# Decoder layer on one core: two more tiles of x copied in and split ahead of the context, the first half of the values' weights ahead of tiles 6 and 7, four column sums behind the weights' split

## Chip, core and metric

The kernel runs on 1 core of one Trainium2 chip. The metric is the device time of one execution in microseconds (us), lower is better.

## What is computed

One decoder layer over x (2 batches x 2048 rows x 512 columns, float32): a self-attention without softmax, a cross-attention to a context of 2 x 154 rows with a mask and a softmax over 16 heads, and a feed-forward step with a gate that mixes each row with the row before it; after each of the three the input is added and the rows are normalised.

```
x = layernorm(x + self_attn(x))            # (q k^T) v, no softmax: no row-by-row score is needed
x = layernorm(x + cross_attn(x, ctx, ctx, mask))   # softmax(q k^T / sqrt(32)) v, 16 heads
x = layernorm(x + ffn(x))                  # sigmoid(xr W_r) * (relu(xk W_k)^2 W_v)
```

Since the self-attention has no softmax, the kernel folds it for each batch into one matrix made of the Gram matrix x^T x and the sums of x's columns. The change is in the part that collects these two and that projects the context to the keys and values of the cross-attention.

## The kernel before

The program has two blocks, `prologue` and `layers`. The prologue (from the start to about 116 us) reads x by rows in 32 tiles of 128 rows, 16 a batch (`HALF`), through a ring of 4 buffers (`RING`). Tile j uses buffer j % 4. Every product with full precision is made of three passes over a high and a low part of each operand, so data that has come in is first split: ScalarE rounds it to the high part, VectorE subtracts that from the raw data.

The program of each engine is written out by hand, in order, and engines meet by semaphores only.

SyncE (`sp_program`) issues the copies. `load(j)` (L188) copies tile j, 256 KB. From tile 4 on it waits until the tile that was in the same buffer has been split (`split_lo`), halved (`halved`) and added to the column sums (`summed`). All copies of SyncE stand in one queue, in program order: tiles 0 to 3, the context (L192, 616 KB), tiles 4 to 7, the first half of the values' weights (L195, 512 KB), the second half (L196, 512 KB), the keys' weights (L197, 1024 KB), the values' bias broadcast to 128 rows (L198), the column biases (L199), then tiles 8 to 19.

ScalarE (`act_program`): `high(j)` makes the high part of tile j (L220) and half of the tile (L221). `part_high(i)` (L245) makes the high part of piece i of what the context's products need: 0 is the context, 1 and 2 are the halves of the values' weights, 3 is the keys' weights. The order is tiles 0 to 4, piece 0, tiles 5 to 7, pieces 1 to 3; then ScalarE issues four copies on its own queue (self_wv, self_bv, self_wk, cross_wq, 1024 KB each except the bias), splits tiles 8 to 11 and copies the keys out of PSUM (L260).

VectorE (`dve_program`): `low(j)` first adds tile j to the column sums `x_sum` (L301, for tiles 0 to 19), then makes the low part of the tile (L305). `part_low(i)` (L335) makes the low part of piece i. The order is tiles 0 to 4, piece 0, tiles 5 to 7, pieces 1, 2, 3, tiles 8 and 9, then the values with their bias out of PSUM (L347, `v_raw`, which gives `v_sum`), then tiles 10 to 17.

GpSimd sums the columns of tiles 20 to 31; its first add waits for tile 19's.

TensorE (`pe_program`): nine warming products, `sums(0..7)` (tiles 0 to 7 into the Gram matrix, L442 and L447), the three products of the values (they wait for `part_lo` of the pieces 0 to 2), the four products of the keys (they wait for piece 3; the second, third and fourth also each wait for one of the three `v_raw` additions, whose PSUM bank they take), then `sums(8..17)` and the rest of the prologue. The products use lines 88 to 90 (`three_pass`). The column sums are read by TensorE only once a batch (`columns`, L464).

`layers` is the main part: 16 groups of 256 rows, a hand-written pipeline over all engines from 116 us to the end. It is not changed.

Of the kernel before, what the change touches and what calls it, by code (L numbers as in the profile page):

```python
# [12 lines left out]
KT = D // P  # L13
# [10 lines left out]
RING = 4  # L24
# [58 lines left out]
def f32(ap):  # L83
    return ap.bitcast(F32)
# [20 lines left out]
def prologue(nc, io, mem, banks, weights, kv, m_in, xt, x_ring, place):  # L105
# [8 lines left out]
    x_in, x_both, x_lo = zip(*x_ring)  # L114
# [4 lines left out]
    ctx_t, w_k, w_v, bv_row, v_raw, x_sum = (place[x] for x in ("ctx_t", "cross_wk", "cross_wv", "bv_row", "v_raw", "x_sum"))  # L119
# [4 lines left out]
    to_split = [[x[:, k, :] for x in whole[i]] for i, k in  # L124
                ((0, slice(0, KT)), (1, slice(0, KT // 2)), (1, slice(KT // 2, KT)), (2, slice(0, KT)))]
# [5 lines left out]
    rows_of = [(r, min(P, B * CTX - r)) for r in range(0, B * CTX, P)]  # L131
    TILES = B * S // P
    HALF = TILES // B
    vector_adds = range(HALF + RING)
    wide = lambda name: io[name].rearrange("(k p) n -> p k n", p=P)
    early = ("cross_wq",) + LATE_WEIGHTS[:-1]

# [19 lines left out]
    with ExitStack() as ctx:  # L157
        flag = lambda name, per=1, step=1: Flag(nc, ctx, name, per, step)
        ctx_in, wv_in, wv_rest_in, wk_in = (
            flag(x, 1, 16) for x in ("ctx_in", "cross_wv_in", "cross_wv_rest_in", "cross_wk_in"))  # L160
        biases_in, ones_set = flag("cross_biases_in", 2, 16), flag("ones_set")
        part_in, part_hi, part_lo = (ctx_in, wv_in, wv_rest_in, wk_in), flag("ctx_parts_hi", 4), flag("ctx_parts_lo", 4)
        x_here = [flag(f"gram_x{i}", 1, 16) for i in range(RING)]
        split_hi, split_lo, halved, summed, gram_mm = (
            flag(x) for x in ("gram_hi", "gram_lo", "gram_half", "gram_sum", "gram_mm"))
        made, zeroed = flag("ident_zeroed"), flag("zeroed", 2)
# [15 lines left out]
        def sp_program(sp):  # L182
            def load(j):
                if j >= RING:
                    sp.wait_ge(*split_lo.at(j - RING))
                    sp.wait_ge(*halved.at(j - RING))
                    sp.wait_ge(*summed.at(j - RING))
                sp.dma_start(x_in[j % RING][:], io["x_rows"][j * P:(j + 1) * P, :]).then_inc(*x_here[j % RING].up)  # L188

            for j in range(RING):  # L190
                load(j)
            sp.dma_start(ctx_t[:], wide("ctx_cols")).then_inc(*ctx_in.up)  # L192
            for j in range(RING, 2 * RING):
                load(j)
            sp.dma_start(w_v[:, 0:KT // 2, :], wide("cross_wv")[:, 0:KT // 2, :]).then_inc(*wv_in.up)  # L195
            sp.dma_start(w_v[:, KT // 2:KT, :], wide("cross_wv")[:, KT // 2:KT, :]).then_inc(*wv_rest_in.up)  # L196
            sp.dma_start(w_k[:], wide("cross_wk")).then_inc(*wk_in.up)  # L197
            sp.dma_start(bv_row[:], io["rows"][3:4, :].broadcast_to([P, D])).then_inc(*biases_in.up)  # L198
            sp.dma_start(col_sb[:], io["cols"]).then_inc(*biases_in.up)  # L199
            for j in range(2 * RING, 5 * RING):  # L200
                load(j)
            sp.wait_ge(*v_sum.at(0))
            sp.wait_ge(*zeroed.at(0))
            for j in range(5 * RING, TILES):
                load(j)
                for dst, src in placements[j - 5 * RING::TILES - 5 * RING]:
                    sp.dma_start(dst, src).then_inc(*placed.up)
            sp.wait_ge(*gram_mm.at(TILES - 1))
            sp.wait_ge(*split_lo.at(TILES - 1))
            sp.wait_ge(*summed.at(TILES - 1))  # L210
            sp.dma_start(xt_in[:], wide("x_cols")[:, :, 0:GT]).then_inc(*xt_here.up)
            sp.wait_ge(*placed.at(0))

        def act_program(act):
            def high(*tiles):
                for j in tiles:
                    act.wait_ge(*x_here[j % RING].at(j // RING))
                    if j >= RING:
                        act.wait_ge(*gram_mm.at(j - RING))
                    act.activation(x_hi[j % RING], by_k(x_in[j % RING]), ACT.Copy).then_inc(*split_hi.up)  # L220
                    act.activation(x_half[j % RING], by_k(x_in[j % RING]), ACT.Copy, scale=0.5).then_inc(*halved.up)  # L221

            def weight_high(i):
                raw, hi, _ = weights[early[i]]
                act.wait_ge(*w_here[early[i]].at(0))
                act.activation(hi[:], raw[:], ACT.Copy).then_inc(*w_high.up)

            def take_sums(b):
                act.wait_ge(*gram_mm.at((b + 1) * HALF - 1))
                for i in range(1, KT, 2):  # L230
                    act.activation(g[b][:, i, :], gram[b][i][:], ACT.Copy).then_inc(*g_act.up)

            def load_weight(name):
                act.dma_start(weights[name][0][:], wide(name)).then_inc(*w_here[name].up)

            def load_square(name):
                act.dma_start(f[name][:], wide(name)).then_inc(*f_here[name].up)

            def load_row(name):
                r = ("self_bk", "self_bv", "self_bo").index(name)  # L240
                act.dma_start(f[name][:], io["rows"][r:r + 1, :].broadcast_to([P, D])).then_inc(*f_here[name].up)

            def part_high(i):
                act.wait_ge(*part_in[i].at(0))
                act.activation(to_split[i][1], to_split[i][0], ACT.Copy).then_inc(*part_hi.up)  # L245

            high(0, 1, 2, 3, 4)
            part_high(0)
            high(5, 6, 7)
            for i in range(1, len(to_split)):  # L250
                part_high(i)
            load_square("self_wv")
            load_row("self_bv")
            load_square("self_wk")
            load_weight(early[0])
            high(8, 9, 10, 11)
            act.wait_ge(*biases_in.at(0))
            for m in range(KT):
                act.wait_ge(*k_mm.at(0, m + 1))
                act.activation(kt[:, m, :], gram[1][(m - 1) % KT][:, 0:B * CTX], ACT.Identity,  # L260
                               bias=bk[:, m:m + 1]).then_inc(*k_ok.up)
            high(12, 13)
            load_row("self_bk")
            high(14, 15, 16, 17)
            take_sums(0)
            load_weight(early[1])
            high(18, 19)
            load_square("self_wo")
            high(20, 21)
            load_square("self_wq")  # L270
            high(22, 23)
            load_row("self_bo")
            for name in early[2:]:
                load_weight(name)
            for i in range(len(early)):
                weight_high(i)
                high(2 * i + 24, 2 * i + 25)
            for q in range(KT):
                act.wait_ge(*u_mm.at(0, q + 1))
                act.activation(u0[:, q, :], u_bank[q][:], ACT.Copy).then_inc(*u_ok.up)  # L280
            take_sums(1)
            act.wait_ge(*xt_here.at(0))
            act.activation(xt_hi[:], xt_in[:], ACT.Copy).then_inc(*xt_high.up)
            for i in range(KT):
                act.wait_ge(*m_mm.at(0, i + 1))
                act.activation(t[0][:, i, :], m_bank[i][:], ACT.Copy).then_inc(*m_out.up)
                act.wait_ge(*m_eye.at(0, i + 1))
                act.activation(m_hi[:, i, :], t[0][:, i, :], ACT.Copy).then_inc(*m_high.up)

        def dve_program(dve):  # L290
            def low(*tiles):
                for j in tiles:
                    i = j % RING
                    if j in vector_adds:
                        b = j // HALF
                        dve.wait_ge(*x_here[i].at(j // RING))
                        if j:
                            dve.wait_ge(*summed.at(j - 1))
                        else:
                            dve.wait_ge(*made.at(1))  # L300
                        dve.tensor_tensor(x_sum[:, b, :], x_sum[:, b, :], x_in[i][:], ALU.add).then_inc(*summed.up)  # L301
                    dve.wait_ge(*split_hi.at(j))
                    if j >= RING:
                        dve.wait_ge(*gram_mm.at(j - RING))
                    dve.tensor_tensor(by_k(x_lo[i]), by_k(x_in[i]), f32(x_hi[i]), ALU.subtract).then_inc(*split_lo.up)  # L305
# [26 lines left out]
            def part_low(i):  # L332
                raw, hi, lo = to_split[i]
                dve.wait_ge(*part_hi.at(0, i + 1))
                dve.tensor_tensor(lo, raw, f32(hi), ALU.subtract).then_inc(*part_lo.up)  # L335

            dve.memset(ones[:], 1.0).then_inc(*ones_set.up)
            low(0, 1, 2, 3, 4)
            part_low(0)
            low(5, 6, 7)  # L340
            for i in range(1, len(to_split)):
                part_low(i)
            low(8, 9)
            dve.wait_ge(*biases_in.at(0))
            for r, (r0, rn) in enumerate(rows_of):
# [1490 lines left out]
```

## Time and profile before

| | us |
|---|---|
| median of 3 runs | 927.82 (927.65 to 927.93) |
| the profiled execution, its own time | 927.58 |
| its span in the trace | 925.8 |
| TensorE (PE) busy | 908.7 (98%) |
| VectorE (DVE) busy | 707.6 (76%) |
| ScalarE (ACT) busy | 545.4 (59%) |
| GpSimd (POOL) busy | 500.9 (54%) |

Times in the trace are microseconds from the start of the span. PE is TensorE's matmuls, PEld its weight loads, SPq and ACTq are the instructions by which SyncE and ScalarE issue copies, q1 is SyncE's DMA queue and q10 ScalarE's. A time in brackets behind a row is how long the engine was idle just before it and what ended that. In a row of copies the last number is the time from issue to landing. TensorE's granted clock is 1.00 in every stretch shown.

### The profile page before, as it was taken

The page shows a single profiled execution, that of the slowest core. Times are in us where ns is not written, and L with a number is a line of the kernel's source. Part 1 is how long each engine was busy: PE and PEld are TensorE (multiplying, and loading weights), DVE is VectorE, ACT ScalarE, POOL GpSimd, SP SyncE. Part 2 cuts the span into 40 slices and gives each one's busy share as a digit, 9 for nine tenths or more (in the row PEclk, how much of TensorE's full clock was granted, in tenths as well). Part 3 has the DMA queues.
Part 4 walks back from the last instruction along what each step waited for, and adds up shares of the span by engine and source line. Part 5 has one row for each costly group of instructions (what it writes and reads, how often), then busy time and mean ns, then how long its engine had stood idle before and what let it go on. Part 6 is the DMA issues. An engine that isn't in the chain of part 4 may idle for free.

```text
span 925.8 us, 18979 instructions
## 1 busy us (share of the span) xinstructions
PE 908.7 (98%) x6694; PEld 730.2 (79%) x6694; DVE 707.6 (76%) x1985; ACT 545.4 (59%) x1658; POOL 500.9 (54%) x505
## 2 busy tenths in 40 slices
PE   8999998999999999999999999999999999999997
PEld 7867566667787878888888787878787878787876
DVE  6697456457797979787887878787878787879775
ACT  6555206657665757575856666656575757575631
POOL 1034015657675666657575756666566665756420
PEclk9999999999999999999999999999999999999999
DMA  8791000103000000002101010101010010100001
GB/s 293 244 336 48 23 26 29 38 8 108 15 24 31 25 31 24 31 24 81 29 25 30 25 30 25 30 25 30 24 29 25 12 43 8 47 1 24 1 23 46
DMA packets 30890, 45.65 MB, mean 49 GB/s; under 512 B 2764, under 2 KB 15564, under 8 KB 30540
## 3 DMA queue, kind: packets, MB, share of 16 engines
q1 hardware_dynamic: 26139, 35.26, 11.9%
q10 hardware_dynamic: 4656, 9.18, 2.9%
q8 instruction: 54, 0.88, 0.4%
q14 instruction: 41, 0.33, 0.1%
HBM read 34.10 MB, written 9.70 MB: 47 GB/s over the span
## 4 chain that ended last, share of the span: by engine, by line
PE 73%; DVE 6%; issue 4%; POOL 3%; ACT 2%; POOLq 0%; DVEq 0%; ACTq 0%
PE dense L88 18%; PE dense L90 17%; PE dense L89 17%; PE turned L1501 5%; PE scores L1489 4%; PE rest_value L1515 3%; PE rest_value L1519 3%; PE turned L1398 1%; PE dense L1398 1%; PE rest_value L1507 1%; PE scores L1404 1%; DVE prob L1041 1%; POOL row_inv L1304 1%; ACT prob L756 1%; PE dense L1443 1%
## 5 line engine op out<-in xcount | busy, mean ns | idle before, releaser
L1304 POOL TENSOR_TENSOR row_inv<-row_sum,minus_one 128x4 f32<-128x4 f32 x128 | 145.6, 1138 | 262.5 <-ACT prob L756 260.9
L756 ACT ACTIVATE prob<-prob,row_min 128x154 f32<-128x154 f32 x512 | 209.4, 417 | 20.4 <-DVE row_min L1041 20.4
L1310 POOL TENSOR_TENSOR prob<-prob,row_inv 128x512 f32<-128x512 f32 x128 | 136.4, 1065 | 0.0
L1041 DVE CUSTOM_DVE_ANT_0 prob<-scores,mask_add 128x154 f32<-128x154 f32 x512 | 127.0, 309 | 6.3 <-PE scores L1489 6.2
L764 ACT ACTIVATE prob_t<-turned 128x512 f32<-128x512 f32 x128 | 75.8, 592 | 53.1 <-PE turned L1501 53.1
L756 ACT ACTIVATION_READ_ACCUMULATOR prob<-prob,row_min 128x1 f32 x512 | 98.8, 193 | 0.0
L1501 PE MATMUL turned<-ident,prob 128*128 128x128 f32 x512 | 77.0, 273 | 3.7 <-POOL prob L1310 1.4
L88 PE MATMUL dense<-xt_hi,cross_wq_hi 128*128 128x256 f32 x256 | 75.2, 294 | 1.3 <-DVE xt_lo L1032 1.3
L88 PE MATMUL dense<-mix_k_hi,ffn_wk_hi 128*128 128x256 f32 x256 | 74.6, 291 | 0.0
L1501 PEld LDWEIGHTS turned<-ident,prob 128*128 128x128 f32 x512 | 61.0, 141 | 15.8 <-issue 4.7
L1099 DVE TENSOR_TENSOR k_act_lo<-square,k_act_hi 128x512 fp32r<-128x512 f32 x32 | 51.4, 1606 | 28.8 <-ACT k_act_hi L789 28.8
L89 PE MATMUL dense<-xt_lo,cross_wq_hi 128*128 128x256 f32 x256 | 72.3, 282 | 0.0
L90 PE MATMUL dense<-xt_hi,cross_wq_lo 128*128 128x256 f32 x256 | 72.3, 282 | 0.0
L90 PE MATMUL dense<-mix_k_hi,ffn_wk_lo 128*128 128x256 f32 x256 | 71.7, 280 | 0.0
L89 PE MATMUL dense<-mix_k_lo,ffn_wk_hi 128*128 128x256 f32 x256 | 71.6, 280 | 0.0
L775 ACT ACTIVATE o_t_hi<-rest_value 128x256 fp32r<-128x256 f32 x64 | 24.5, 383 | 76.2 <-PE rest_value L1519 76.2
L1032 DVE TENSOR_TENSOR xt_lo<-dense,xt_hi 128x512 fp32r<-128x512 f32 x32 | 22.0, 689 | 49.6 <-ACT xt_hi L740 49.6
L1309 POOL TENSOR_TENSOR prob_rest<-prob,row_inv 128x104 f32<-128x104 f32 x128 | 53.5, 418 | 10.0
L1489 PEld LDWEIGHTS scores<-kt,q 32*128 32x128 f32 x1024 | 36.8, 184 | 26.2 <-issue 25.9
L88 PE MATMUL dense<-cross_wo_hi,o_t_hi 128*128 128x512 f32 x128 | 53.3, 417 | 0.0
L88 PE MATMUL dense<-m_hi,xt_hi 128*128 128x512 f32 x128 | 51.9, 405 | 0.5 <-PEq L541 0.3
L1489 PE MATMUL scores<-kt,q 32*128 32x154 f32 x1024 | 51.6, 315 | 0.3 <-DVE row_min L1041 0.3
(273 smaller groups left out, 2658.9 us busy)
## 6 DMA issues: line engine op xcount, KB each, us to landing
x_rows<-x_rows SPq DMA_DIRECT2D x32, 256.0 KB, 4.4
xt_raw<-x_cols SPq DMA_DIRECT2D x16, 512.0 KB, 3.7
out<-gate_then_y SPq DMA_DIRECT2D x15, 512.0 KB, 2.8
mask_in<-mask SPq DMA_DIRECT2D x16, 154.0 KB, 2.3
cross_wv<-cross_wv SPq DMA_DIRECT2D x2, 512.0 KB, 6.8
cross_wk<-cross_wk SPq DMA_DIRECT2D x1, 1024.0 KB, 9.3
self_wv<-self_wv ACTq DMA_DIRECT2D x1, 1024.0 KB, 8.0
self_wk<-self_wk ACTq DMA_DIRECT2D x1, 1024.0 KB, 11.8
```

The costliest lines, as they stand in the source:

```text
L88: pe.matmul(out, sta[0], mov[0], start=first, stop=False, skip_group_check=True)
L89: pe.matmul(out, sta[0], mov[1], start=False, stop=False, skip_group_check=True)
L90: return pe.matmul(out, sta[1], mov[0], start=False, stop=last, skip_group_check=True)
L756: m = act.activation(keys, keys, ACT.Exp, bias=row_min[:, buf, t, h:h + 1], scale=-1.0, accum_out=row_sum[:, buf, t, h:h + 1])
L764: act.activation(pt[:, 0:HPG, t * P:(t + 1) * P], t_bank[:].rearrange("p (c n) -> p c n", c=HPG), ACT.Copy).then_inc(*t_out.up)
L1041: m = dve.tensor_tensor_reduce(prob[buf][:, t, h * CTX:(h + 1) * CTX], s_bank[:, h, t * CTX:(t + 1) * CTX], mask_add[n % 2][:, t, :], -SCA ...
L1099: dve.tensor_tensor(ka_lo[:, kt2, :], square[:, kt2, :], f32(ka_hi[:, kt2, :]), ALU.subtract).then_inc(*ka_lo_ok.up)
L1304: pool.tensor_tensor(row_inv[:, buf, t, :], row_sum[:, buf, t, :], minus_one[:], ALU.pow).then_inc(*p_inv.up)
L1309: pool.tensor_tensor(after, keys[:, :, P:CTX], inv.broadcast_to([P, HPG, CTX - P]), ALU.mult)
L1310: pool.tensor_tensor(keys[:, :, 0:P], keys[:, :, 0:P], inv.broadcast_to([P, HPG, P]), ALU.mult).then_inc(*p_norm.up)
L1489: m = pe.matmul(s_bank[:, h, t * CTX:(t + 1) * CTX], q[rows, g, t * P:(t + 1) * P], kt[rows, g, b * CTX:(b + 1) * CTX], start=True, stop=T ...
L1501: m = pe.transpose(t_bank[:, h * P:(h + 1) * P], prob[g % 2][:, t, h * CTX:h * CTX + P], ident[:])
```

## The change

It moves instructions and adds or removes none.

SyncE issues tiles 4 and 5 ahead of the context, then the context, then the first half of the values' weights, then tiles 6 and 7, and the rest as before. ScalarE and VectorE split tile 5 ahead of the context instead of behind it. VectorE no longer adds tiles 4 to 7 to the column sums in front of their split, but all four in a row between the split of the values' weights (piece 2) and that of the keys' weights (piece 3). `load(8)` to `load(11)` wait for these additions (`summed`), since they overwrite the buffers.

```diff
-    vector_adds = range(HALF + RING)
+    vector_adds, late_adds = range(HALF + RING), range(RING, 2 * RING)
 ...
-            for j in range(RING):
+            for j in range(RING + 2):
                 load(j)
             sp.dma_start(ctx_t[:], wide("ctx_cols")).then_inc(*ctx_in.up)
-            for j in range(RING, 2 * RING):
+            sp.dma_start(w_v[:, 0:KT // 2, :], wide("cross_wv")[:, 0:KT // 2, :]).then_inc(*wv_in.up)
+            for j in range(RING + 2, 2 * RING):
                 load(j)
-            sp.dma_start(w_v[:, 0:KT // 2, :], wide("cross_wv")[:, 0:KT // 2, :]).then_inc(*wv_in.up)
             sp.dma_start(w_v[:, KT // 2:KT, :], wide("cross_wv")[:, KT // 2:KT, :]).then_inc(*wv_rest_in.up)
 ...
-            high(0, 1, 2, 3, 4)
+            high(0, 1, 2, 3, 4, 5)
             part_high(0)
-            high(5, 6, 7)
+            high(6, 7)
 ...
+            def add(*tiles):
+                for j in tiles:
+                    b, i = j // HALF, j % RING
+                    dve.wait_ge(*x_here[i].at(j // RING))
+                    if j:
+                        dve.wait_ge(*summed.at(j - 1))
+                    else:
+                        dve.wait_ge(*made.at(1))
+                    dve.tensor_tensor(x_sum[:, b, :], x_sum[:, b, :], x_in[i][:], ALU.add).then_inc(*summed.up)
+
             def low(*tiles):
                 for j in tiles:
                     i = j % RING
-                    if j in vector_adds:
 ...
+                    if j in vector_adds and j not in late_adds:
+                        add(j)
 ...
-            low(0, 1, 2, 3, 4)
+            low(0, 1, 2, 3, 4, 5)
             part_low(0)
-            low(5, 6, 7)
-            for i in range(1, len(to_split)):
-                part_low(i)
+            low(6, 7)
+            part_low(1)
+            part_low(2)
+            add(*late_adds)
+            part_low(3)
             low(8, 9)
```

## Rows read from the trace of the kernel before

**Rows 1.** The page: the span, and TensorE's busy time, share and matmuls.
```profile
span 925.8 us, 18979 instructions
PE 908.7 (98%) x6694; PEld 730.2 (79%) x6694; DVE 707.6 (76%) x1985; ACT 545.4 (59%) x1658; POOL 500.9 (54%) x505
```

**Rows 2.** Waits of TensorE up to 140 us: total, times, longest, in us.
```profile
PE scores L442 <- DVE x_rows_lo L305: 1.6, 1, 1.6
PE dense L88 <- PEq L541: 0.3, 1, 0.3
```

**Rows 3.** Timeline of TensorE, 12 to 30 us: start, us, engine, line, operation.
```profile
12.37 0.28 PE L447 MATMUL scores<-x_rows_both 128*128 128x256 f32 x1
14.27 0.50 PE L442 MATMUL scores<-x_rows_lo,x_rows_both 128*128 128x512 f32 x1 [1.62 <-DVE x_rows_lo L305]
...
18.96 0.50 PE L88 MATMUL turned<-cross_wv_hi,ctx_t_hi 128*128 128x512 f32 x1
...
27.46 0.30 PE L88 MATMUL dense<-ctx_t_hi,cross_wk_hi 128*128 128x308 f32 x1
...
29.15 0.30 PE L88 MATMUL turned<-ctx_t_hi,cross_wk_hi 128*128 128x308 f32 x1
```

**Rows 4.** Timeline of VectorE, 11 to 26 us.
```profile
11.56 1.44 DVE L335 TENSOR_TENSOR ctx_t_lo<-ctx_t,ctx_t_hi 128x1232 fp32r<-128x1232 f32 x1 [0.95 <-ACT ctx_t_hi L245]
12.92 0.69 DVE L301 TENSOR_TENSOR x_sum<-x_sum,x_rows 128x512 f32<-128x512 f32 x1
13.52 0.69 DVE L305 TENSOR_TENSOR x_rows_lo<-x_rows,x_rows_both 128x512 fp32r<-128x512 f32 x1
...
16.54 2.38 DVE L335 TENSOR_TENSOR cross_wv_lo<-cross_wv,cross_wv_hi 128x1024 fp32r<-128x1024 f32 x2
21.17 2.29 DVE L335 TENSOR_TENSOR cross_wk_lo<-cross_wk,cross_wk_hi 128x2048 fp32r<-128x2048 f32 x1 [2.26 <-ACT cross_wk_hi L245]
...
25.79 0.68 DVE L347 TENSOR_TENSOR v_raw<-turned,bv_row 128x512 f32<-128x512 f32 x1
```

**Rows 5.** Timeline of ScalarE and of its own issues, 15 to 20 us.
```profile
15.25 1.06 ACT L245 ACTIVATE cross_wv_hi<-cross_wv 128x1024 fp32r<-128x1024 f32 x1 [0.60 <-DMA cross_wv<-cross_wv]
16.59 1.06 ACT L245 ACTIVATE cross_wv_hi<-cross_wv 128x1024 fp32r<-128x1024 f32 x1 [0.28 <-DMA cross_wv<-cross_wv]
...
19.23 0.43 ACTq L237 DMA_DIRECT2D self_wv<-self_wv  x1
```

**Rows 6.** SyncE's issues of tiles 4, 5 and 8, from timelines of narrow windows.
```profile
4.76 0.34 SPq L188 DMA_DIRECT2D x_rows<-x_rows  x1
5.97 0.33 SPq L188 DMA_DIRECT2D x_rows<-x_rows  x1
...
12.72 0.47 SPq L188 DMA_DIRECT2D x_rows<-x_rows  x1
```

**Rows 7.** Copies by issue: size, us to landing, of tiles 0, 4, 5, 8, 12.
```profile
x_rows<-x_rows SPq DMA_DIRECT2D x1, 256.0 KB, 2.6
...
x_rows<-x_rows SPq DMA_DIRECT2D x1, 256.0 KB, 4.5
...
x_rows<-x_rows SPq DMA_DIRECT2D x1, 256.0 KB, 3.9
...
x_rows<-x_rows SPq DMA_DIRECT2D x1, 256.0 KB, 8.2
...
x_rows<-x_rows SPq DMA_DIRECT2D x1, 256.0 KB, 6.4
```

**Rows 8.** Busy time by stretch; the last two columns are DMA share and GB/s.
```profile
5.50:9.50 4.00, 4.00 (x26) 3.52 (x25) 3.23 (x6) 2.52 (x6) 0.00 (x0) 1.00 1.00 352
9.50:12.00 2.50, 2.50 (x16) 2.21 (x16) 1.55 (x3) 2.50 (x5) 0.00 (x0) 1.00 0.79 258
12.00:15.50 3.50, 1.88 (x11) 1.41 (x10) 3.50 (x6) 2.90 (x7) 0.00 (x0) 1.00 1.02 328
```

More of the change, by code:

```diff
@@ L293, in low @@
                     i = j % RING
-                    if j in vector_adds:
[L295 to L301, printed above, removed]
+                    if j in vector_adds and j not in late_adds:
+                        add(j)
                     dve.wait_ge(*split_hi.at(j))
```

## Prediction

> **What bounds the kernel now.** I read the page first. TensorE is busy for 908.7 of 925.8 us [rows 1], so only work or idle time on TensorE's own path can move the end. The change adds no work there, so the next view is TensorE's waits in the stretch that ends after the prologue. Apart from its start there are two: 1.6 us for a low part of x on VectorE, and 0.3 us between the blocks, which the change doesn't touch [rows 2]. The timeline of TensorE then places the 1.6 us: the last matmul of tile 4 starts at 12.37 and takes 0.28, so it ends at 12.65, and tile 5 starts at 14.27 [rows 3]. Tiles 5, 6 and 7 then run without a gap to the values' product at 18.96, so a tile costs (18.96 - 14.27) / 3 = 1.56 us [rows 3]. From there to the end of the prologue TensorE has no wait, so any time by which the values' product starts earlier is handed on, as long as nothing behind it becomes late.
>
> The reader should then ask what else ends at 18.96. VectorE's timeline answers: the two low parts of the values' weights run from 16.54 for 2.38 us, to 18.92 [rows 4]. So the values' product has two conditions, the end of tile 7 on TensorE and the split of the weights, and in this trace they end within 0.04 us of each other. ScalarE had waited for both halves of the weights to land (0.60 and 0.28 us idle) and took up the second at 16.59 [rows 5]. The stall of 1.6 us is thus covered by a copy that is equally late: removing it alone gives nothing.
>
> **The change part by part. The stall at tile 5.** Before, VectorE does the context's low part (1.44 us from 11.56) and tile 5's addition (from 12.92) ahead of tile 5's low part at 13.52 [rows 4]. After, tile 5 is split first. Tile 5 was issued at 5.97 and landed 3.9 us later, at 9.87, with the context in front of it; with the queue nearly empty a tile takes 2.6 us, which gives 8.6 [rows 6, 7]. Even from 9.87 on, behind tile 4's two activations on ScalarE, the high and low parts (0.6 and 0.69) end at about 11.6, ahead of the 12.65 at which TensorE wants them. The stall goes. TensorE would then want tile 6 at 14.21, tile 7 at 15.77 and the values at 17.34, so the most that can be won is 18.96 - 17.34 = 1.62 us. The least of this part alone is nothing.
>
> **The order of the copies.** The second half of the values' weights has exactly the same bytes in front of it as before. From its landing the way is the same too: 18.92 - 16.59 = 2.33 us for the high part and what is left of the low parts [rows 4, 5]. So the values start at the later of 17.34 and the landing plus 2.33. What the order can change is how well the queue is fed. Before, the queue moved 352 GB/s from 5.5 to 9.5 us, 258 from 9.5 to 12 with the engines 79% busy, and 328 after [rows 8]: the dip lies where SyncE was waiting for buffers of tiles 6 and 7 and had not yet issued the weights. After, the first half of the weights is issued ahead of tile 6's wait, about 2 us earlier, and that dip should be filled. On the other side the context is issued only behind tile 5, at about 6.3 instead of ahead of tile 4's issue at 4.76 [rows 6], so the queue may run dry between tile 3 and tile 5.
>
> An estimate of the landing: a lone tile's 2.6 us [rows 7] are 0.75 us for 262 thousand bytes at 352 GB/s [rows 8] and 1.85 us of way. From tile 5 to the second half of the weights 2.47 MB are to move. At the mean of the three stretches, 320 GB/s, this gives 5.97 + 1.85 + 7.7 = 15.5; with the dip filled at 340 GB/s, 15.05. The same reckoning of the trace before, with what was then still queued (about 2.58 MB at 5.97), gives 15.9 where 16.55 was seen, so I add 0.65 and get 15.7 to 16.15. I take 15.9. The ends are 14.8 (352 GB/s throughout, nothing added) and 17.4 (258 throughout).
>
> **The splits behind it.** Tiles 6 and 7 now stand behind the context and half the weights. By the same reckoning tile 7 lands at about 13.7. ScalarE then has its two activations (1.05) and two halves of the weights at 1.06 [rows 5]: 16.85 if it never waits, then 1.2 for the last low part, 18.05. That is just inside what the landing gives, 15.9 + 2.33 = 18.23. Tile 7's low part is ready by about 15.1, ahead of 15.77. If tile 7 lands later than 14.4, TensorE stalls on it, but the weights' split behind it sets the start anyway. So the values start at about 18.25: a gain of 0.7 us of the possible 1.62.
>
> **The four additions.** They cost VectorE 0.60 us each [rows 4], as before. Two of them leave the way to the low parts of tiles 4 to 7; all four now stand ahead of the keys' low part. From 18.25 they end at 20.65. The keys' low part could not start before 21.17, since it waited 2.26 us for ScalarE [rows 4], so it stays near 21.2 to 23.5, and the keys' product wants it at 27.46 less the gain [rows 3]. Cost nothing, with more than 3 us of cover. If that cover were gone each addition would cost 0.60.
>
> **Tiles 8 to 11.** This is a queue that the change moves past others. Tile 8 was issued at 12.72 [rows 6]; it now waits for tile 4's addition and goes at about 18.9, tile 9 at 19.5, close to ScalarE's own 3 MB of copies that begin at 19.23 [rows 5]. On VectorE tiles 8 and 9 stand ahead of the values' bias additions, which ran from 25.79 [rows 4], and the second keys' product wants the first of these at 29.15 [rows 3], after the change at 28.45. From tile 9's landing they need 0.60 + 0.60 + 0.68. Between 2.6 us (tile 0, alone) and 8.2 us (tile 8, with the keys' weights in front) [rows 7], tile 9 would land at 22.1 to 27.7. I take 6.4 us, of tile 12, which went in the middle of ScalarE's copies [rows 7]: 25.9, bias out at 27.8, 0.65 us of cover. Cost nothing, with an end at 29.6 - 28.45 = 1.15 us. Tiles 10 and 11 and all that follows stand behind TensorE's seven products of values and keys and have several us. The sums of columns are first read at about 54 us, and GpSimd's first addition waits for tile 19's, which is paced by TensorE; both move with TensorE.
>
> **Sum.** 0.7 us less on the profiled execution: span 925.1, its own time 927.58 - 0.7 = 926.9. That execution is 0.24 us below the median, so the median becomes 927.82 - 0.7 = 927.1 us.
>
> **Rivals.** (a) The whole stall is won: the weights land by 15.0, which 352 GB/s would give (14.8), and the values start at 17.35. For it speaks the filled dip, against it that tile 7's and the weights' splits on ScalarE alone need until 18.05 unless tile 7 lands by 13.0. Time 926.2. (b) The weights land when they did, 16.5, since the same bytes are in front: 927.8. For it speaks that the ends of two chains met before and only one is shortened; against it the dip at 9.5 to 12 us. The Trainium skill, "DMA: Bandwidth & Descriptors", in "Queues, rings and completion order", says that each DMA engine takes its descriptors in ring order: by that rule alone a new order changes who lands first and not when the last one does, which is this rival. (c) Slower: tile 9 lands late. If its copy takes 8.2 us as tile 8's did, the second keys' product waits 1.15 us for the bias addition, and with 0.7 won before it the sum is 0.45 slower, 928.3. It decides from a landing of tile 9 after 26.6. The row for it is tile 8's 8.2, the row against it that tile 8 had the keys' weights in front, which now are ahead of its issue. (d) Slower: the queue runs dry without the context. 631 thousand bytes at 352 GB/s are 1.8 us of work missing between tile 3 and tile 5, of which tile 4 fills 0.75. The weights land 1.05 later, at 17.6, the values start at 19.95, 1.0 slower, 928.8. It decides when the rate from 5.5 to 9.5 us falls under about 290 GB/s.
>
> **How the numbers follow.** The forecast (0.35 to 1.2 us won) has 0.42, (a) 0.13, (b) 0.22, (c) 0.12, (d) 0.11. The range for 8 in 10 takes in (a)'s near side, (b) and (c) and half of (d): 926.1 to 928.6. A measurement of this kernel can tell about 0.2%, 1.86 us, from no change. No case gets there: the whole stall is 1.62. What is left is what I have not seen in the trace, a wait in the main part that shifts, or (c) and (d) together: 0.03 faster, 0.05 slower, 0.92 within.
>
> **What would show it.** Right: no wait of TensorE at tile 5; tiles 4 and 5 landed by 9 us; the second half of the weights landed at 15.7 to 16.2; the values' product started near 18.25 with its wait ended by the weights' low part; over 300 GB/s from 9.5 to 12 us; tiles 8 and 9 issued near 19 and landed by 26; no wait at the keys' products. Wrong: a wait at the second keys' product (c), a rate under 290 GB/s before 9.5 us (d), or any new wait of TensorE between 35 and 115 us, where I have reckoned that everything only moves along.

## The result and the profile after

The changed kernel takes 928.87 us in the median of 20 runs (927.74 to 931.41), the kernel before 927.65 (926.74 to 928.06, 20 runs beside it). The medians are 1.2 us apart. The ratio, which goes by all runs and not by the medians, is 1.0017, 95% interval 1.001 to 1.0024, or 0.9 to 2.2 us: slower. The median is just beyond the upper end of the range that was forecast (928.6), and on the other side of the likeliest case (0.7 us faster). One run of all that are reported here, of the kernel with the sums in place, took 1279.13 us at a granted clock of 0.655 and is left out of its ratio.

The profiled execution of the changed kernel took 930.53 us, one of the slowest of its 20, so its trace shows more loss than the median has. The page opens with a span 2.9 us longer, as against [rows 1]:

```profile
span 928.7 us, 18979 instructions
PE 910.0 (98%) x6694; PEld 730.5 (79%) x6694; DVE 708.4 (76%) x1985; ACT 545.7 (59%) x1658; POOL 501.5 (54%) x505
```

TensorE's waits up to 140 us, which answer to [rows 2]:

```profile
PE turned L88 <- DVE v_raw L353: 1.3, 1, 1.3
PE scores L448 <- DVE x_rows_lo L309: 1.1, 1, 1.1
PE turned L88 <- DVE cross_wv_lo L339: 0.9, 1, 0.9
PE dense L88 <- PEq L547: 0.3, 1, 0.3
```

One wait of 1.6 us has become three: at a tile (1.1), ahead of the values' product (0.9) and at the second keys' product (1.3). TensorE's timeline places them, beside [rows 3]. Its first rows are tile 0's first matmuls:

```profile
4.91 0.77 PE L448 MATMUL scores<-x_rows_lo,x_rows_both 128*128 128x512 f32 x1
5.49 0.63 PE L453 MATMUL scores<-x_rows_both 128*128 128x256 f32 x2
5.91 0.63 PE L448 MATMUL scores<-x_rows_lo,x_rows_both 128*128 128x512 f32 x1
6.34 0.36 PE L453 MATMUL scores<-x_rows_both 128*128 128x256 f32 x1
6.53 0.39 PE L448 MATMUL scores<-x_rows_lo,x_rows_both 128*128 128x512 f32 x1
...
14.70 0.28 PE L453 MATMUL scores<-x_rows_both 128*128 128x256 f32 x1
16.11 0.51 PE L448 MATMUL scores<-x_rows_lo,x_rows_both 128*128 128x512 f32 x1 [1.14 <-DVE x_rows_lo L309]
...
20.30 0.50 PE L88 MATMUL turned<-cross_wv_hi,ctx_t_hi 128*128 128x512 f32 x1 [0.87 <-DVE cross_wv_lo L339]
...
31.96 0.41 PE L88 MATMUL turned<-ctx_t_hi,cross_wk_hi 128*128 128x308 f32 x1 [1.33 <-DVE v_raw L353]
```

Where TensorE lost the 2.9 us can be read here. The second keys' product starts at 31.96 instead of 29.15, 2.81 later, and nothing more is lost behind it. Tile 5 ends at 14.98; before it would have ended at 12.65 + 1.56 = 14.21 without its stall. These 0.77 us come from the start: the first matmuls take 0.63 to 0.77 us instead of 0.39 to 0.50 until 6.3 us. Then tile 6, not tile 5, is waited for (1.14), tiles 6 and 7 take 3.31 instead of 3.13 (0.18), and the values' product waits 0.87. Against the 1.62 of before this makes 0.77 + 1.14 + 0.18 + 0.87 - 1.62 = 1.34 at the values' product, which is 20.30 - 18.96. The wait of 1.33 at the second keys' product and 0.14 of starting up again behind it make up the rest. The 0.77 of the slow start does not belong to the change: of the twelve traces of the experiments below three start as slowly, three for one or two matmuls and six not at all, and a second trace of the changed kernel is among the six.

These terms say where TensorE was idle or slow. They don't say what set the end. The bias addition came out at 31.23 + 0.68 = 31.91, and it hung on tile 9's landing and not on TensorE: had TensorE lost nothing ahead of it, it would have waited there for longer, and the second keys' product would still have started at about 31.96. A second trace of the same kernel, shown below, bears this out. It starts fast and loses more at tile 6 and less at the bias addition, and its second keys' product starts at 31.89, with the same span of 928.7 us. What decides in these traces is the 31.91 at which the addition is out.

The work ahead of the values, on ScalarE and VectorE, beside [rows 4, 5]:

```profile
12.68 1.24 ACT L245 ACTIVATE ctx_t_hi<-ctx_t 128x1232 fp32r<-128x1232 f32 x1 [2.52 <-DMA ctx_t<-ctx_cols]
14.71 0.63 ACT L220 ACTIVATE x_rows_both<-x_rows 128x512 fp32r<-128x512 f32 x1 [0.79 <-DMA x_rows<-x_rows]
...
16.80 1.99 ACT L245 ACTIVATE cross_wv_hi<-cross_wv 128x1024 fp32r<-128x1024 f32 x2
19.34 0.42 ACTq L237 DMA_DIRECT2D self_wv<-self_wv  x1
...
20.16 3.07 DVE L299 TENSOR_TENSOR x_sum<-x_sum,x_rows 128x512 f32<-128x512 f32 x4
23.15 2.28 DVE L339 TENSOR_TENSOR cross_wk_lo<-cross_wk,cross_wk_hi 128x2048 fp32r<-128x2048 f32 x1
28.51 0.69 DVE L299 TENSOR_TENSOR x_sum<-x_sum,x_rows 128x512 f32<-128x512 f32 x1 [3.08 <-DMA x_rows<-x_rows]
...
31.23 0.68 DVE L353 TENSOR_TENSOR v_raw<-turned,bv_row 128x512 f32<-128x512 f32 x1
```

ScalarE waits for the context and for tile 6, then works without a gap from 14.71 through tiles 6 and 7 and both halves of the weights to 18.79. VectorE waits until 28.51 for tile 8, does tiles 8 and 9, and only then the bias addition at 31.23 for which TensorE is waiting. Before, that addition ran at 25.79.

SyncE's issues of tiles 8 and 9, and by issue the copies of the second half of the values' weights, tile 8 and tile 9 (size, us to landing), beside [rows 6, 7]:

```profile
20.93 0.33 SPq L188 DMA_DIRECT2D x_rows<-x_rows  x1
21.73 0.40 SPq L188 DMA_DIRECT2D x_rows<-x_rows  x1
```

```profile
cross_wv<-cross_wv SPq DMA_DIRECT2D x1, 512.0 KB, 7.8
...
x_rows<-x_rows SPq DMA_DIRECT2D x1, 256.0 KB, 7.6
...
x_rows<-x_rows SPq DMA_DIRECT2D x1, 256.0 KB, 8.2
```

Tile 9 lands at 21.73 + 8.2 = 29.9. The second half of the weights, issued at 8.84, lands at 16.6, as it did before. The stretches that answer to [rows 8]:

```profile
5.50:9.50 4.00, 4.00 (x23) 3.56 (x22) 3.61 (x6) 3.86 (x8) 0.00 (x0) 1.00 0.74 226
9.50:12.00 2.50, 2.50 (x16) 2.21 (x15) 0.69 (x1) 0.65 (x2) 0.00 (x0) 1.00 1.04 377
12.00:15.50 3.50, 2.98 (x18) 2.39 (x16) 1.55 (x2) 2.03 (x3) 0.00 (x0) 1.00 1.02 346
```

The queue runs partly dry ahead of the context (226 GB/s instead of 352) and makes it up behind (377 instead of 258).

### The profile page after: what moved, and what is told of

The parts are those of the page before. It is cut to its first block, busy times and chain, and to the rows that moved or that the text cites. A ratio compares the mean times of both kernels' runs of the same rounds, so it can differ in the third digit from the quotient of the medians.

```text
span 928.7 us, 18979 instructions
## 1 busy us (share of the span) xinstructions
PE 910.0 (98%) x6694; PEld 730.5 (79%) x6694; DVE 708.4 (76%) x1985; ACT 545.7 (59%) x1658; POOL 501.5 (54%) x505
## 4 chain that ended last, share of the span: by engine, by line
PE 73%; DVE 6%; issue 4%; POOL 3%; ACT 2%; POOLq 0%; DVEq 0%; ACTq 0%
PE dense L88 18%; PE dense L90 17%; PE dense L89 17%; PE turned L1507 5%; PE scores L1495 4%; PE rest_value L1521 3%; PE rest_value L1525 3%; PE turned L1404 1%; PE dense L1404 1%; PE rest_value L1513 1%; PE scores L1410 1%; DVE prob L1047 1%; POOL row_inv L1310 1%; ACT prob L762 1%; PE dense L1449 1%
## 5 line engine op out<-in xcount | busy, mean ns | idle before, releaser
L1495 PEld LDWEIGHTS scores<-kt,q 32*128 32x128 f32 x1024 | 36.8, 184 | 26.2 <-issue 25.9
```

Of the source, the lines that this page charges most:

```text
L1495: m = pe.matmul(s_bank[:, h, t * CTX:(t + 1) * CTX], q[rows, g, t * P:(t + 1) * P], kt[rows, g, b * CTX:(b + 1) * CTX], start=True, stop=T ...
```

## The experiments

Each median stands beside that of the kernel before, run on the same chip in the same turn; ratios have their 95% interval, and since they go by all runs they can differ from the ratio of the medians. The first theory was that the late column sums cost: they free the buffers late, so tiles 8 to 11 are issued late, tile 9 lands late, and the bias additions behind it on VectorE hold up the keys' product. Its rival was that the new order of copies costs, by the queue that runs dry ahead of the context.

### Which part of the change costs

**Late sums only.** The kernel before with the four additions moved.

```diff
-            for i in range(1, len(to_split)):
-                part_low(i)
+            part_low(1)
+            part_low(2)
+            add(*late_adds)
+            part_low(3)
```

> The kernel before with one part of the change: VectorE's four column sums of tiles 4 to 7 stand behind the split of the values' weights; copies and splits keep their old order. Theory 1 (the late sums delay the issue of tiles 8 to 11 to about 19.7 to 21.5 us, tile 9 lands near 29.5 us, and the values' bias additions behind tile 9 on VectorE hold the second keys' product): a wait of TensorE at the first bias addition of 1.5 to 2.3 us, time 1.4 to 2.2 us above before (929.1 to 929.8). Theory 2 (the loss comes from the copies' order and the queue that runs dry): no such wait, time within 0.3 us of before, 927.4 to 928.0.

Measured: 927.79 against 927.50, ratio 1.0004 (0.9995 to 1.0013). The runs spread from 926.58 to 929.30, as many as three of 11 at 929.0 or above. The profiled one was one of these three (929.29), and its only waits of TensorE beside the two at the ends are

```profile
PE turned L88 <- DVE v_raw L353: 1.4, 1, 1.4
...
PE turned L88 <- DVE cross_wv_lo L339: 1.0, 1, 1.0
```

The stall at tile 5 is gone in this trace too: the tile's low part no longer stands behind an addition, and TensorE's matmuls had started slowly by some 0.6 us. It wins nothing: the values' product waits for the weights instead and starts at 18.95, where it started at 18.96 before.

```profile
18.95 0.50 PE L88 MATMUL turned<-cross_wv_hi,ctx_t_hi 128*128 128x512 f32 x1 [1.01 <-DVE cross_wv_lo L339]
```

So the mechanism of theory 1 is there, in its size too, but the median moves by only 0.3 us where 1.4 to 2.2 were expected. The late sums alone hardly explain 1.2 us, which is the very end of their interval.

**All but the late sums.** The changed kernel with each addition back in front of its tile's split.

> The changed kernel with the four column sums put back in front of each tile's split. Theory 1: tiles 8 to 11 issued from about 14 to 17 us, no wait at the keys' products; left is the later start of the values' product, some 0.6 us: 927.9 to 928.4. Theory 2: the time stays at that of the changed kernel, 928.9 within 0.3.

Measured: 927.44 against 927.50, ratio 1.0004 (0.9995 to 1.0013), no change. In its trace tile 6 is waited for by 0.8 us and the values by 0.3, and they start at 18.62. The queue is as dry as in the changed kernel and catches up in the same way:

```profile
5.50:9.50 4.00, 4.00 (x26) 3.52 (x25) 4.00 (x7) 3.86 (x9) 0.00 (x0) 1.00 0.81 224
9.50:12.00 2.50, 2.50 (x17) 2.24 (x16) 1.30 (x3) 1.53 (x3) 0.00 (x0) 1.00 1.06 400
```

The new order of copies by itself moves the median neither way, and theory 2, which wanted 928.9, falls. Whether the order costs a few tenths stays open: three of its ten other runs took 928.7 to 929.6, the ratio stands for 0.4 us, and that is as much as for the late sums alone.

**Tiles 4 and 5 first, the weights at their old place, sums in place.**

> Only tiles 4 and 5 ahead of the context, in the copies and in the splits; the values' weights behind tiles 6 and 7 and the sums in front of each split, as before. Theory 1: tiles 6 and 7 land near 13.2 and 13.9 us, the stall at tile 5 is gone, the second half of the weights lands at 16.5 as in both kernels and the values' product starts near 18.95: 927.4 to 928.0. Theory 2 (the queue that runs dry ahead of the context costs all): about 1 us slower, 928.6.

Measured: 927.55 against 927.50, ratio 1.0000 (0.9991 to 1.0009). The stall at tile 5 became one of 0.93 us at a later tile, and the values' product started at 18.92:

```profile
15.44 0.50 PE L447 MATMUL scores<-x_rows_lo,x_rows_both 128*128 128x512 f32 x1 [0.93 <-DVE x_rows_lo L309]
18.92 0.51 PE L88 MATMUL turned<-cross_wv_hi,ctx_t_hi 128*128 128x512 f32 x1 [0.18 <-DVE cross_wv_lo L339]
```

**Only the splits' order, all copies and sums as before.**

> Only the order of the splits: tile 5 ahead of the context on ScalarE and VectorE; all copies and sums as before. Theory 1 (the values' weights, not tile 5, set the start of the values' product): the wait of 1.6 us at tile 5 goes and about 1 us comes back at tile 6 behind the context's low part; the values' product still starts at 18.9 to 19.0, time 927.4 to 927.9. Rival: the wait is worth its length and the time falls by over 1 us, under 926.6.

Measured: 927.45 against 927.50, ratio 0.9998 (0.9989 to 1.0006). In the profiled execution (926.50) the wait at tile 5 is gone and none came at tile 6, contrary to what was expected there; the values' product started at 17.96, since the weights had landed 1.5 us earlier in that execution than in the trace of before. The median agrees with theory 1: taking the visible stall away is worth nothing that can be measured.

### What holds the keys' product

**The changed kernel once more.**

> The changed kernel once more, for a comparison on one chip with the three that follow. Theory 1 (tile 9 lands late behind ScalarE's copies and the bias additions wait behind it): a wait of over 1 us at the second keys' product, tile 9 landed near 29.9 us, time 1.0 to 1.5 above before. If the time is within 0.3 of before, the difference lay in the chip or the day.

Measured: 928.67 against 927.65, ratio 1.0013 (1.0004 to 1.0021). The loss is there again. Tile 9 lands at 29.8, as expected; the wait behind it is shorter than expected, since TensorE comes later. Its trace (930.54) has two waits, 2.10 us at tile 6 and 0.74 at the bias addition, and a stretch at a lower clock. First two stretches, then TensorE's timeline:

```profile
16.00:18.00 2.00, 1.79 (x10) 1.61 (x11) 0.87 (x3) 2.00 (x4) 0.00 (x0) 0.93 0.93 350
18.00:20.00 2.00, 2.00 (x8) 1.71 (x8) 2.00 (x2) 1.41 (x2) 0.00 (x0) 0.50 0.10 30
```

```profile
16.21 0.50 PE L448 MATMUL scores<-x_rows_lo,x_rows_both 128*128 128x512 f32 x1 [2.10 <-DVE x_rows_lo L309]
...
18.79 0.63 PE L448 MATMUL scores<-x_rows_lo,x_rows_both 128*128 128x512 f32 x1
...
31.89 0.41 PE L88 MATMUL turned<-ctx_t_hi,cross_wk_hi 128*128 128x308 f32 x1 [0.74 <-DVE v_raw L353]
```

The granted clock (the third last column) is 0.50 from 18 to 20 us, TensorE's lower level of 1.2 GHz (narrower stretches show it at 1.00 until 17.6, at 0.50 from 17.8 to 21.0 and back at 1.00 from 21.2), and a matmul of 512 columns takes 0.63 instead of 0.39 us. Ahead of it the engine had been idle for 2.10 us. Tiles 6 and 7 took 20.71 - 16.21 = 4.5 us instead of 3.13, 1.4 us more. Of this at most 0.4 reached the values' product, since the low parts of its weights ended at 20.34 in this trace, and none of it the second keys' product, which started when the bias addition was out (31.84). The kernel before, with an idle time of 1.62, shows 1.00 in every stretch.

**The bias additions ahead of tiles 8 and 9.** The changed kernel with one block moved on VectorE:

```diff
-            low(8, 9)
             dve.wait_ge(*biases_in.at(0))
             for r, (r0, rn) in enumerate(rows_of):
                 ...
+            low(8, 9)
```

> The changed kernel with the three bias additions of the values ahead of tiles 8 and 9 on VectorE; copies, splits and late sums as in the change. Theory 1: tile 9 is as late as before (28.5 to 30 us), but the keys' products don't wait; time 1.0 to 1.4 below the changed kernel, 927.4 to 928.0. Rival (the loss lies ahead of the values' product, at tile 6): no gain, 928.6 to 929.2.

Measured: 927.52 against 927.65, ratio 0.9998 (0.9989 to 1.0007), and 1.15 below the changed kernel of the same turn. Tile 9 is nearly as late as ever (issued at 20.51, 8.7 us to landing, so 29.2), and VectorE takes it up only behind the biases, at 29.58.

```profile
27.77 0.68 DVE L352 TENSOR_TENSOR v_raw<-dense,bv_row 52x512 f32<-52x512 f32 x1 [2.10 <-PE dense L90]
28.38 0.68 DVE L299 TENSOR_TENSOR x_sum<-x_sum,x_rows 128x512 f32<-128x512 f32 x1
28.98 0.68 DVE L309 TENSOR_TENSOR x_rows_lo<-x_rows,x_rows_both 128x512 fp32r<-128x512 f32 x1
29.58 0.68 DVE L299 TENSOR_TENSOR x_sum<-x_sum,x_rows 128x512 f32<-128x512 f32 x1
```

The late landing by itself cost nothing that can be measured; what cost was the order of VectorE's program, with an urgent addition behind a late tile. TensorE's waits ahead of the values' product, the rival, are still there in this trace (0.4 and 0.9 us), and the loss is gone.

**ScalarE's copies later.** The changed kernel, its four copies on ScalarE's queue behind `high(8, 9, 10, 11)`.

```diff
+            high(8, 9, 10, 11)
             load_square("self_wv")
             load_row("self_bv")
             load_square("self_wk")
             load_weight(early[0])
-            high(8, 9, 10, 11)
```

> The changed kernel with ScalarE's four copies (self_wv, self_bv, self_wk, cross_wq) issued behind the splits of tiles 8 to 11. Theory 1, in its part on the queues: tile 8 lands at some 23.5 us and tile 9 at 24.3 although they are issued as late as in the change, no wait at the keys' products, 927.4 to 928.0. Rival (the late issue by itself makes them late): tile 9 lands after 27 us and the wait stays.

Measured: 927.38 against 927.65, ratio 0.9999 (0.9990 to 1.0008), no wait at the keys' products. Tile 8 was issued at 19.09 and took 2.6 us to land. The copies of a stretch from SyncE's issue of tile 8 on, first in this kernel (19 to 24 us), then in the changed one (20.9 to 25 us); the rows are the queues' packets and the issues of the stretch with their us to landing:

```profile
q1 hardware_dynamic: 570, 1.04, 69.8%
issues: line engine op xcount, KB each, median us to landing
x_rows<-x_rows SPq DMA_DIRECT2D x4, 256.0 KB, 2.9
```

```profile
q10 hardware_dynamic: 594, 1.18, 79.0%
issues: line engine op xcount, KB each, median us to landing
cross_wq_raw<-cross_wq ACTq DMA_DIRECT2D x1, 1024.0 KB, 13.7
x_rows<-x_rows SPq DMA_DIRECT2D x4, 256.0 KB, 8.5
```

In the changed kernel SyncE issued tiles 8 to 11 in this stretch and its queue q1 moved nothing for 4.1 us: every packet is ScalarE's (q10). With ScalarE's copies out of the way the same tiles take 2.9 us. The Trainium skill, "DMA: Bandwidth & Descriptors", in "Queues, rings and completion order", has each DMA engine take turns between the queues for which it has work; by that the tiles would have begun to move soon after their issue, at half the rate. These rows don't show it for the first 4 us. Not all of the 4.1 us is the other queue's doing: with ScalarE's queue empty tile 8's first packet moved 1.0 us after its issue (20.1 in this kernel). In the changed kernel it moved at 25.3, when ScalarE's queue had moved 1.3 MB, about the size of its first two copies (1024 and 256 KB); from 26 to 30 us the two queues moved about as much each (91 to 106 packets against 104 to 113 in a us).

### What the late sums need in order to cost

**Tiles 4 and 5 first and late sums, the weights behind tile 7 again.**

> The changed kernel with the first half of the values' weights issued behind tile 7 again; tiles 4 and 5 ahead of the context and the late sums stay. Theory (the late sums cost when the weights' split ends over 3 us behind their landing, which the place of tiles 4 and 5 brings about on ScalarE and not the place of the weights): 928.2 to 928.9, a wait of TensorE at the bias addition. Rival (the early first half is what makes the sums late, by moving tiles 6 and 7 back): within 0.4 of before, 927.3 to 928.0.

Measured: 927.78 against 927.55, ratio 1.0001 (0.9992 to 1.0010). The theory was wrong and the rival right: with the weights at their old place the late sums cost 0.2 us in the median, as in the first experiment, and the profiled execution (927.01) waits 0.23 at the bias addition. The rows are the issues of ScalarE's first copy (self_wv) and of SyncE's tile 8, first in this kernel, then in the one with late sums only:

```profile
17.98 0.43 ACTq L237 DMA_DIRECT2D self_wv<-self_wv  x1
...
18.27 0.33 SPq L188 DMA_DIRECT2D x_rows<-x_rows  x1
```

```profile
19.23 0.42 ACTq L237 DMA_DIRECT2D self_wv<-self_wv  x1
...
19.58 0.33 SPq L188 DMA_DIRECT2D x_rows<-x_rows  x1
```

Tile 8 goes out 0.3 us behind ScalarE's first copy in both, and 1.6 us behind in the changed kernel (19.34 and 20.93), by when ScalarE has issued all four of its copies. Tile 8 then lands after 5.1 and 5.2 us, and after 7.6 in the changed kernel. But the bias addition stands behind tile 9, and tile 9's copy takes much the same in all three, 7.4, 8.2 and 8.2 us. What differs there is when it is issued, 19.07, 20.38 and 21.73, and so when it lands: 26.5, 28.6 and 29.9.

The issue follows the sums, and the sums follow the weights' split. With the weights ahead of tiles 6 and 7, tile 6 lands at 14.6 instead of 11.4 in this kernel. ScalarE then works through tiles 6 and 7 and both halves of the weights in one go, and the weights' split, behind which the late sums stand, ends 3.6 us behind the weights' landing (20.24 - 16.6), against 2.33 before. How late tile 6 is differs by execution, though: in six traces with the changed order of copies ScalarE took it up between 12.9 and 14.8.

### Versions that beat both

**The values' products in two halves.** Tile 5's split first, and TensorE takes the first half of the weights as soon as that half is split:

```diff
-            pe.wait_ge(*part_lo.at(0, 3))
-            for r, (r0, rn) in enumerate(rows_of):
-                for k in range(KT):
+            for part in range(2):
+                pe.wait_ge(*part_lo.at(0, 2 + part))
+                for r, (r0, rn) in enumerate(rows_of):
+                    for k in range(part * KT // 2, (part + 1) * KT // 2):
                         ...
```

> Tile 5's split ahead of the context (as in the run with only that), and the values' products in two halves: those with the first half of the weights wait only for that half's split, the rest for the second; all copies and sums as in the kernel before. Theory 1 (the second half's landing sets the start of the values' product and hides the stall): the values' product starts at 17.4 to 18.0 us in every execution, time 926.2 to 926.9. Rival (nothing ahead of the values' product matters): 927.4 to 927.8.

Measured: 926.97 against 927.65, ratio 0.9991 (0.9982 to 1.0000). In its trace the wait ahead of the values is gone and one of 0.6 us at tile 6 is left, so the values' product starts at 18.38, later than the 17.4 to 18.0 expected. The halves alone, with tile 5's split at its old place, were not run. Again:

> The kernel with tile 5's split ahead of the context and the values' products in two halves, once more. 926.6 to 927.2, 0.5 to 0.9 below before.

Measured: 926.95 against 927.63, ratio 0.9990 (0.9981 to 0.9999).

**The same with the late sums and the biases ahead of tiles 8 and 9**, copies in the old order:

> Copies in the order of the kernel before. Tile 5 split ahead of the context, the four column sums behind the weights' split, the three bias additions ahead of tiles 8 and 9, the values' products in two halves. Theory 1: late sums cost nothing once nothing urgent stands behind tile 9 on VectorE, and they take 1.2 us of VectorE's work out of the way of tiles 6 and 7, so the 0.6 us wait at tile 6 goes as well: 926.0 to 926.8. Rival (late sums cost by themselves): above 927.3.

Measured: 926.69 against 927.63, ratio 0.9987 (0.9978 to 0.9996). No wait of TensorE is left in the prologue between its warming products and the end of the block, and the values' product starts at

```profile
17.63 0.50 PE L88 MATMUL turned<-cross_wv_hi,ctx_t_hi 128*128 128x512 f32 x1
```

which is 1.33 us earlier than before.

**The whole change, with halves and the biases first:**

> The whole change (its order of copies too) with the three bias additions ahead of tiles 8 and 9 and the values' products in two halves. Theory 1: tile 6 lands near 13 us in this order, so a wait of 0.4 to 1.1 us at tile 6 stays and only the wait in front of the values' product goes: 926.6 to 927.4, and slower than the kernel with the old order of copies. Rival (feeding the first half of the weights early is what counts): below that kernel.

Measured: 926.61 against 927.63, ratio 0.9990 (0.9981 to 0.9999). A wait of 0.9 us at tile 6 is left in its trace, as expected; that it would be slower than the old order of copies was not seen (926.61 and 926.69). With the bias additions first and the weights' wait split, the change does no harm.

## Why the prediction was wrong, point by point

**The bound.** Right: TensorE's path alone decides, the stall of 1.6 us was covered by the weights' split, and its removal alone was worth nothing measurable (split order only, 927.45 against 927.50). The late sums alone show the same: no stall, and the values at 18.95. The traces with the old order of copies differ in when the weights land, though, 15.0 to 16.6 us, and with an early landing the stall is worth up to 1 us in that execution.

**The stall at tile 5.** Right that it goes in the changed kernel. Tiles 4 and 5 landed by 9 us.

**The landing of the weights.** The step put 15.9; 16.6 was measured, just as before. The mechanism was half right: the dip at 9.5 to 12 us was filled (377 GB/s), but it was paid for by the dry queue ahead of the context, which stood among the rivals (226 GB/s, under the 290 named there). Rival (b), ring order, has the right landing for this execution. One execution can't tell between the cases, though: in six traces with the new order of copies the landing lay between 14.9 and 16.8, about as wide as with the old one. That is more than the 0.6 us between the 15.9 of the forecast and (b)'s 16.5.

**The splits behind the copies.** This step failed in its size, by 2 us in this trace. It took tile 7's landing at 13.7 and the values' start at 18.25. Tile 6 landed at 14.6 and tile 7 at about 15.3, and the values began at 20.30. From tile 6's arrival ScalarE and VectorE need 5.5 us in a row (14.71 to 20.24), in three other traces of this order too (12.9 to 18.4, 13.5 to 19.0, 14.8 to 20.3). So the start of the values was set by tile 6, which now stood behind the context and half the weights, and no longer by the weights. The sum had counted only tile 7's two activations behind its landing; tile 6 came so late that all four stood in a row.

**The four additions.** "Cost nothing, with more than 3 us of cover" holds for VectorE's own time: the keys' low part ended at 25.4, ahead of the keys' product. What failed is what the additions release.

**Tiles 8 to 11.** The step that failed and decided: the late issue of tile 9 was put at "cost nothing", with the bias addition out at 27.8 and 0.65 us of cover. It was out at 31.91, and TensorE waited 1.33 us for it; with the addition moved ahead of tiles 8 and 9 the loss is gone (927.52 against 928.67). Two terms were wrong. Tile 9's issue was put at 19.5 and came at 21.73, since the sums stood behind a weights' split that ended 2 us later than reckoned. And 6.4 us was taken for the copy, the middle, where 8.2 was measured. Tile 9 so landed at 29.9 and not at 25.9. The mechanism of rival (c) was right, tile 9 late and the bias addition behind it. That its price for the copy, 8.2 us, is the number measured is luck: the tile from which it was taken had the keys' weights in front of it on its own queue, and here the other queue's copies were in the way. The cost should have been in the forecast: the cover was 0.65 us with a range of 5.6 us on one of its terms.

**The sum.** Forecast 927.1 with 928.6 as the upper end; (c) had 0.12 and (d) 0.11, and they were taken one at a time. In the traces they are not independent: the order of copies that delays tile 6 also delays the sums, and so tile 9's issue. The single experiments point the same way without proving it: late sums alone +0.3 and +0.2 us in the medians, the order of copies with the sums in place -0.1, both together +1.0 and +1.2; but the intervals of the single parts reach up to 1.2 us. The chances by 0.2% (same 0.92) held: 0.17%.

What stays open: the median loss can't be split exactly into the wait at the bias addition and the rest, since single executions differ by up to 3.7 us. That the wait for the bias addition is at least most of it follows from the two kernels that avoid it, the additions first and ScalarE's copies later, 1.15 and 1.29 us faster than the changed one in the same turn. Both profiled executions of the changed kernel were among its longest (930.5), so what a median one looks like wasn't seen. The dropped clock was seen in one trace; how often it comes is not known. Why SyncE's queue stood still for 4 us behind ScalarE's is not known either.

## What to carry to other kernels

When a small job is moved back, cost what it releases, not its own time: here four additions of 0.60 us with 3 us of cover freed four buffers late, and the copies into them then went out behind another queue's and landed late. In a program written out in order, ask of every engine which urgent instruction stands behind one that waits for a copy; moving three additions ahead of that wait made the lateness harmless. When waits follow each other on one engine, don't add them up as costs: the last one, if it ends at a time set elsewhere, swallows those ahead of it. And when two chains end within 0.04 us of each other, shorten the one that isn't seen as a wait too: taking the stall away gave nothing alone and about 0.7 us with a values' product that could begin on half its weights.

## What the runs showed of the hardware

- Two queues did not share from the start. Tiles 8 and 9, issued on SyncE's queue 1.6 and 2.4 us behind ScalarE's first copy, moved no byte for 4.1 us and landed after 7.6 and 8.2 us; with ScalarE's queue empty the first packet came after 1.0 us and the copies took 2.6 to 2.9 us. Issued 0.3 us behind ScalarE's first copy, tile 8 took 5.1 and 5.2 us, and tile 9, 0.8 us later, took 7.4 and 8.2.
- The landing of one copy differs by execution: the second half of the values' weights, issued at 8.7 to 8.9 us in the new order of copies, landed between 14.9 and 16.8 in six traces.
- After an idle time of 2.10 us on TensorE the granted clock fell to 0.50, some 1.5 us after the work had begun again, and stayed there for 3.2 us (17.8 to 21.0); tiles 6 and 7 took 1.4 us longer. After 1.62 us in the kernel before it did not fall.
- TensorE's first matmuls behind the warming products took 0.63 to 0.77 us in some executions and 0.39 to 0.50 in others of kernels that are alike up to there, with 1.00 in the column of the granted clock.
